# Stages of a tile two quads apart, three or four tiles to a group, and one-hots behind the steps of a slot, in a one-core graph, attention and slice-token kernel

## The reference, cut to what matters

```python
edge_index = jnp.stack([src, dst])                     # 100,000 edges, 6,250 nodes
xn = _layernorm(x, axis=-1)                            # x: 6250 x 256
x = x + gnn(xn, edge_index, ...) + mix(xn[None], ...)[0]
x = x + ffn(_layernorm(x, axis=-1)[None], ...)[0]

def _gnn_layer(x, row, col, W, b, g, beta):            # twice, W0 then W1
    neigh = x[col]
    agg = segment_sum(neigh, row, num_segments=n)      # sums of gathered rows
    h = (x + agg / deg) @ W.T + b
    hn = (h - mu) * rsqrt(var + EPS) * g + beta
    return silu(hn)
# ffn: logits -> softmax over 64 slices and 8 heads -> slice tokens -> attention -> back
slice_weights = softmax((x_mid @ W_slice + b_slice) / temp, axis=-1)
slice_token = einsum('bhnc,bhng->bhgc', fx_mid, slice_weights)
```

## Time and profile before

| | |
|---|---|
| time, median of 3 | 3014.8 us (3012.59 to 3029.4) |
| the profiled execution | 3023.39 us, span 3021.6 us |
| mean granted TensorE clock | 0.867 |
| busy share PE, PEld, DVE, ACT, POOL | 75%, 54%, 50%, 53%, 50% |
| gathers, all on POOL | 1568 |

### The profile page before, as it was taken

One profiled execution on the slowest core, in us unless ns is written; L12 is line 12 of the kernel. 1 busy time (PEld: TensorE's weight loads), 2 busy tenths in 40 slices (PEclk: granted clock), 3 DMA queues, 4 the chain that ended last, 5 costly groups with the idle time before them and its releaser, 6 DMA issues.

```text
span 3021.6 us, 35181 instructions
## 1 busy us (share of the span) xinstructions
PE 2264.3 (75%) x9037; PEld 1622.0 (54%) x9037; DVE 1504.1 (50%) x3513; ACT 1600.5 (53%) x3861; POOL 1522.8 (50%) x1591
## 2 busy tenths in 40 slices
PE   2376588778788788787669476768787877778699
PEld 1253366556565565565545354545454645555368
DVE  8899835555555555556127613343433334345511
ACT  5220276667667667666626465464554555565322
POOL 0000376566555656657740577576756676674000
PEclk9687699998999899999887787989887988889889
DMA  7110133233232333323361444243424343343322
GB/s 177 34 51 0 50 111 100 84 96 96 88 89 87 97 90 101 99 86 101 111 147 52 121 121 142 87 142 94 139 75 133 97 139 114 111 134 91 87 54 60
DMA packets 132041, 293.68 MB, mean 97 GB/s; under 512 B 31098, under 2 KB 76506, under 8 KB 128975
## 3 DMA queue, kind: packets, MB, share of 16 engines
q0 software_dynamic: 75584, 208.18, 23.6%
q1 hardware_dynamic: 17266, 44.84, 5.6%
q10 hardware_dynamic: 39000, 38.41, 4.2%
HBM read 259.31 MB, written 32.00 MB: 96 GB/s over the span
## 4 chain that ended last, share of the span: by engine, by line
PE 46%; DVE 25%; ACT 9%; POOL 8%; issue 7%; DMA 3%; ACTq 1%; DVEq 1%; SPq 0%; POOLq 0%
PE ps L1222 15%; POOL whole L671 8%; PE ps L1241 7%; DVE whole L1942 5%; PE ps L1376 4%; PE ps L1471 3%; DVE arena_a L1553 3%; ACT arena_b L782 3%; PE ps L1258 3%; DVE arena_a L1554 3%; PE ps L1381 2%; DMA arena_b<-mix_rows 2%; PE ps L1310 2%; PE ps L1239 1%; ACT whole L784 1%
## 5 line engine op out<-in xcount | busy, mean ns | idle before, releaser
L671 POOL DMA_INDIRECT whole<-table,arena_a x1568 | 1513.7, 965 | 1010.4 <-issue 457.1
L1222 PE MATMUL ps<-whole 128*125 x3968 | 1024.7, 412 | 210.3 <-issue 85.0
L1222 PEld LDWEIGHTS ps<-whole 128*125 128x125 f32 x3968 | 797.0, 205 | 394.2 <-issue 262.4
L1888 DVE TENSOR_TENSOR whole<-ps,whole 125x257 f32 (+1 forms) x496 | 210.4, 424 | 1091.7 <-PE ps L1222 1069.5
L782 ACT ACTIVATE arena_b<-iota_row,arena_a 128x125 f32<-128x125 f32 (+1 forms) x1984 | 600.4, 387 | 98.5 <-PE ps L1222 46.6
L784 ACT ACTIVATE whole<-arena_b,ones 128x1000 f32<-128x1000 f32 (+1 forms) x248 | 279.9, 1129 | 8.1
L1241 PE MATMUL ps<-arena_b,whole 128*125 128x384 f32 x400 | 225.9, 704 | 0.0
L1239 PE MATMUL ps<-arena_b,ones 3*125 3x384 bf16 x100 | 46.3, 463 | 164.8 <-ACTq L825 164.8
L1942 DVE RECIPROCAL whole<-whole 125x512 f32<-125x512 f32 x50 | 167.7, 3353 | 1.7
L812 ACT ACTIVATE whole<-whole 125x512 f32<-125x512 f32 x50 | 31.6, 631 | 251.4 <-DVE whole L1946 251.4
L1239 PEld LDWEIGHTS ps<-arena_b,ones 3*125 3x125 bf16 x100 | 15.3, 153 | 233.5 <-issue 233.5
(11 more groups left out here) (437 smaller groups left out, 3133.2 us busy)
## 6 DMA issues: line engine op xcount, KB each, us to landing
whole<-table,arena_a POOLq DMA_INDIRECT x1568, 2.8
table<-whole SPq DMA_DIRECT2D x9, 1120.0 KB
whole<-table ACTq DMA_DIRECT2D x50, 125.0 KB
mix_rows<-whole ACTq DMA_DIRECT2D x50, 125.0 KB
arena_a<-table ACTq DMA_DIRECT2D x50, 125.0 KB
arena_b<-in_x_dram ACTq DMA_DIRECT2D x50, 125.0 KB
arena_b<-mix_rows ACTq DMA_DIRECT2D x50, 125.0 KB
x_rows<-whole ACTq DMA_DIRECT2D x50, 125.0 KB
```

The costliest lines, as they stand in the source:

```text
L671: pool.indirect_dma_start(gat[:, GRP * slot + k, 0:D], None, table[l], bass.IndirectOffsetOnAxis(ap=s_dst[:, n:n + 1], axis=0)).then_inc(s ...
L1222: mm = pe.matmul(ps[0:PT, banks[at % len(banks)], 0:width], onehot[:, ROUND * (r % 2) + QS * k + n, :], gat[:, bass.ds(slots[QS * k + n], ...
L1888: dve.tensor_tensor(to, ps[0:PT, banks[at % len(banks)], 0:width].unsqueeze(1), to, ALU.add).then_inc(s("agg_added"), 1)
```

## The change

1. **The plan.** `GROUPS` goes from six tiles to four and, at the end, fewer: 16 groups in place of 12. A tick below 215 is "even": there a stage needs its predecessors two ticks back or more, not one, and a stage (other than S, R, V, Q) comes at most every fourth tick, not every tick. The costs are other numbers, the PE limit is 2.2 in place of 2.3, the DVE limit 2.4 while there are quads and 3.5 after, in place of 3.1.
2. **One-hots on ACT, layer two.** They stand behind the tick's steps and `move_rows`. The first four `Abs` of group tick/2 + 2 come in the even tick, the other four and the `Relu` in the odd one.
3. **`move_rows`** is called for the tick two before, not one.
4. **One-hots on ACT, layer one.** Two groups come ahead of slot 0, and group h + 2 comes behind slot h.

```diff
-GROUPS = [6, 6, 6, 6, 6, 6, 5, 4, 2, 1, 1, 1]
+GROUPS = [4] * 10 + [3, 2, 2, 1, 1, 1]
-PE_COST = {"W": 1.9, "L": 1.0, "D": 0.35, "H": 1.4, "T": 0.35}
-DVE_COST = {"N": 1.6, "M": 1.5, "X": 1.8, "Z": 1.1, "S": 1.5, "V": 1.5, "B": 0.45, "U": 0.6}
+PE_COST = {"W": 1.6, "L": 2.1, "D": 0.6, "H": 1.6, "T": 0.6}
+DVE_COST = {"N": 1.6, "M": 1.4, "X": 1.9, "Z": 1.0, "S": 1.3, "V": 1.3, "B": 0.45, "U": 0.5, "R": 0.2, "Q": 0.4}
+EVEN_UNTIL = 215
+EVEN_PACE = 4
+        even = tick < EVEN_UNTIL
+        dve_room = 2.4 if tick < NQ else 3.5
-                if any(at.get(one, tick) >= tick for one in need):
+                if any(at.get(one, tick) + (1 if even else 0) >= tick for one in need):
                     break
-                if items and (pe + PE_COST.get(st, 0) > 2.3 or dve + DVE_COST.get(st, 0) > 3.1):
+                if st not in "SRVQ" and k and tick - at[st, k - 1] < (EVEN_PACE if even else 1):
                     break
-                if any(s0 == st for s0, _ in items) and st not in "SRVQ":
+                if items and (pe + PE_COST.get(st, 0) > 2.2 or dve + DVE_COST.get(st, 0) > dve_room):
                     break
...
+                def first_half(grp):
+                    for k in range(GRP // 2):
+                        act.activation(away_b[:, k, :], iota_row[:, :], ACT.Abs, bias=s_row[:, grp * GRP + k:grp * GRP + k + 1])
+
-                    for k in range(GRP):
+                    for k in range(GRP // 2 if rest else 0, GRP):
...
-                    window(onehots_ahead, mix_slot)
+                    for grp in range(AHEAD):
+                        onehots(grp)
+                    for half in range(HALVES):
+                        if half < SLOTS:
+                            mix_slot(half)
+                        onehots_ahead(half)
...
-                        if tick % 2 == 0 and tick // 2 + AHEAD < NSG:
-                            onehots(tick // 2 + AHEAD)
                         set_up(tick)
                         for st, k in items:
                             second_step(st, k)
-                        for st, k in PLAN[tick - 1] if tick else []:
+                        for st, k in PLAN[tick - 2] if tick >= 2 else []:
                             move_rows(st, k)
+                        if tick // 2 + AHEAD < NSG:
+                            if tick % 2 == 0:
+                                first_half(tick // 2 + AHEAD)
+                            else:
+                                onehots(tick // 2 + AHEAD, rest=True)
```

More of the change, by code:

```diff
@@ L81 @@
 FED = {"tok": 1, "osT": 2, "attn": 3}
-GROUPS = [6, 6, 6, 6, 6, 6, 5, 4, 2, 1, 1, 1]
+GROUPS = [4] * 10 + [3, 2, 2, 1, 1, 1]
 assert sum(GROUPS) == NT
 STAGES = ("W", "N", "M", "L", "D", "C", "Q", "V", "X", "Z", "R", "S", "B", "H", "T", "U")
-PE_COST = {"W": 1.9, "L": 1.0, "D": 0.35, "H": 1.4, "T": 0.35}
-DVE_COST = {"N": 1.6, "M": 1.5, "X": 1.8, "Z": 1.1, "S": 1.5, "V": 1.5, "B": 0.45, "U": 0.6}
+AFTER = {"T": "U", "H": "T", "B": "H", "X": "Z", "D": "C", "L": "D", "M": "L", "N": "M", "W": "N", "R": "S", "Q": "V"}
+PE_COST = {"W": 1.6, "L": 2.1, "D": 0.6, "H": 1.6, "T": 0.6}
+DVE_COST = {"N": 1.6, "M": 1.4, "X": 1.9, "Z": 1.0, "S": 1.3, "V": 1.3, "B": 0.45, "U": 0.5, "R": 0.2, "Q": 0.4}
 X1_RING, BASE_RING, XL_RING = 3, 3, 3
+EVEN_UNTIL = 215
+EVEN_PACE = 4
 def second_layer_plan():
@@ L98, in second_layer_plan @@
     counts = {st: len(GROUPS) if st in "SRVQ" else NT for st in STAGES}
-    before = {"T": "U", "H": "T", "B": "H", "X": "Z", "D": "C", "L": "D", "M": "L", "N": "M", "W": "N", "R": "S", "Q": "V"}
     last_of = {"S": "B", "V": "X"}
     group_first = {"Z": "R", "C": "Q"}
-    room = {("U", 2): "T", ("Z", 2): "X", ("C", XL_RING): "W", ("T", 1): "H"}
+    room = {"U": (2, "T"), "Z": (2, "X"), "C": (XL_RING, "W"), "T": (1, "H")}
     tick = 0
     while nxt["W"] < NT:
+        even = tick < EVEN_UNTIL
+        dve_room = 2.4 if tick < NQ else 3.5
         pe, dve, items = 0.0, 0.0, []
@@ L109, in second_layer_plan @@
                 need = []
-                if st in before:
-                    need.append((before[st], k))
+                if st in AFTER:
+                    need.append((AFTER[st], k))
                 if st in last_of:
@@ L115, in second_layer_plan @@
                     need.append((group_first[st], group_of[k]))
-                for (other, n), done in room.items():
-                    if other == st and k >= n:
-                        need.append((done, k - n))
-                if any(at.get(one, tick) >= tick for one in need):
+                if st in room and k >= room[st][0]:
+                    need.append((room[st][1], k - room[st][0]))
+                if any(at.get(one, tick) + (1 if even else 0) >= tick for one in need):
                     break
@@ L774, in _, with onehots @@
             for l in range(2):
-                def onehots(grp, l=l):
+                def first_half(grp):
+                    for k in range(GRP // 2):
+                        act.activation(away_b[:, k, :], iota_row[:, :], ACT.Abs, bias=s_row[:, grp * GRP + k:grp * GRP + k + 1])
+                def onehots(grp, rest=False, l=l):
                     made = (grp - RG + 1) * (GRP // QS) + NQ * l
@@ L787, in onehots_ahead @@
                 def onehots_ahead(half):
-                    if half == 0:
-                        for grp in range(AHEAD):
-                            onehots(grp)
                     if half + AHEAD < NSG:
@@ L992, in _ @@
                             second_step(st, k)
-                        for st, k in PLAN[tick - 1] if tick else []:
+                        for st, k in PLAN[tick - 2] if tick >= 2 else []:
                             move_rows(st, k)
-                    assert all(st not in "UX" for st, k in PLAN[-1])
+                        if tick // 2 + AHEAD < NSG:
[3 more added lines that the diff above has]
+                                onehots(tick // 2 + AHEAD, rest=True)
+                    assert all(st not in "UX" for items in PLAN[-2:] for st, k in items)
             act.wait_ge(s("tail_made"), 1)
```

## The result

The changed kernel takes 2914.8 us (median of four runs, 2911.82 to 2919.37) against 3013.7 us for the kernel before on the same chip: a ratio of 0.9664 [0.9634, 0.9694], or 99 us less. The forecast was 2920, from a sum of 97 us less. The profiled execution took 2919.37 us with a span of 2917.3 and a mean granted clock of 0.879. In the changed file the gather is L674, SP's wait for used slots L617, the quads L1234, and the stages T, H, D, L and W on PE are L1368, L1372 and L1374, L1380, L1386 and L1388, and L1393. The columns of the first view are those of the earlier trace rows: the stretch of the quads, from there to the last W, and the end of the ffn.

The account below looks back on a forecast made before the run. POOL's gathers were taken as layer two's floor, 981 us, with only 105 us of stops to win. 105 us gained in the quads minus 8 us behind them made 97 us: 3014.8 - 97 = 2918, taken as 2920; low 2896, high 2980.

Parts of the forecast that it names:

- POOL's stops: Layer two's gathers: POOL's 104.6 us of waits on SP's free slots fall to 10 us, bounds 0 and 50.
- The last quads: End of layer two's quads: they end 14 us after POOL instead of 24, at 2692 us; bounds 10 and 24.
- After the quads: Stretch from the last quad to the last W: 8 us longer than its 75 us, bounds 0 and +25.
- Table loads: ACT in layer two: 54 loads instead of 40, 18 us more, hidden by ACT's slack.
- One-hots: ACT in layer two, one-hots placed behind the steps: 0 us, bounds -5 and +10.
- `move_rows`: ACT's queue issues, all one tick later: 0 us; next user at least ten ticks on in the even part.
- Layer one: ACT's one-hot order in layer one: 0 us in the stage's 1157 us, bounds -5 and +5.
- A: Layer two's quads: PE becomes the limit, 200 of its 260 us idle remain, 2963 us in all; chance 0.15.
- B: Layer two's quads: ACT's copies of T, H and D come late, 3053 us in all; chance 0.07.
- C: Layer two's gathers: a quarter slow down, costing 102 us, so no change at 3015 us; chance 0.06.
- the forecast's own range: Whole kernel: 2896 us (no stops, 10 us of last quads, no longer end) to 2950 us; forecast's chance 0.72.
- 153 us of waits in four kinds: PE in layer two's quads: waits of L on M, T on U and ACT's copies, 153 of 260 us idle, removed.

Follow-up runs that it names:

- ACT's part alone: Kernel before, old plan kept, with ACT's new one-hot order in both layers and move_rows two ticks back: 3067.37 us, ratio 1.0152.
- L and M apart: Kernel before, planner placing a tile's L only after the tick of the previous tile's M, D not ahead of that L: 2903.26 us, ratio 0.9621.
- plan-only kernel: Changed plan with ACT's order and move_rows of the kernel before: 2917.24 us, ratio 0.9658 to the kernel before.

## Why the prediction was right, point by point

**POOL's stops.** The main term, 104.6 us less 10, measured 104.6 less 0.6. POOL is done with its last gather at 2677.1 us (2676.2 + 0.95); forecast 2678. Yet I had left 10 us of stops, so 9 us are missing elsewhere. POOL's group in layer two, of the kernel before and of the changed one, shows where:

```profile
L671 POOL DMA_INDIRECT whole<-table,arena_a x784 | 749.1, 956 | 469.7 <-issue 232.5 <-DMA table<-whole 132.6 <-SPq L614 104.6
```

```profile
L674 POOL DMA_INDIRECT whole<-table,arena_a x784 | 750.7, 958 | 370.8 <-issue 237.9 <-DMA table<-whole 132.2 <-SPq L617 0.6
```

A stop in the list of waits is the whole gap between two gathers, its ordinary 0.30 us included. With the 21 stops went none of these gaps: issue rose from 232.5 to 237.9 us. That is 5.4 us that I took out with the stops and that stays, 1.6 us are in the gathers, and 1.2 us in the start of the stream (1687.9 against 1686.7). The two errors nearly cancel; that the end of POOL came out within 1 us is luck.

**The last quads.** 10.5 us behind POOL (2687.6 against 2677.1), at the good bound of 10 and not the 14 taken.

**After the quads.** +4.8 us, forecast +8, bounds 0 and +25. The one more W was right, but three more L and D are left, not two more L (40 and 28 records of L's 512 columns; 163 on PE in place of 135). PE's busy time still rose by only 4.8 us, since its records ran shorter, W's 414 ns in the mean in place of 495. With a spread from 61.1 us to 75.0 at almost the same count in other runs, that +8 came near is partly luck.

**Table loads.** 54 as counted, hidden as forecast; 32 loads take no less time. The Trainium skill (ScalarE: Activation LUTs, Table sets: the hidden batching unit) advises to batch by table set. Here that gained nothing (0.9668 with 32 loads, 0.9664 with 54); ACT is busy 604 of 984 us.

**One-hots.** 0 us forecast and 0 measured, alone on the old plan (0.9986, on the slower chip) and, together with `move_rows`, with the new one (0.9658 without, 0.9664 with). ACT's waits for the x2 store, which I said would go, are still 10.8 and 5.6 us; they cost nothing.

**`move_rows`.** 0 is right with the changed plan, and only there. The reason that I gave, that the next user is ten ticks on in the even part, fits both: it is eleven or more there, and three in 20 places of the old plan, where the same edit costs 1.8%. (The even part repeats itself every 40 ticks, eight tiles, and not every 20 and four as given ahead.)

**Layer one.** The records of layer one's quads start from 379.8 to 1563.9 us against 378.8 to 1562.2, 0.7 us longer; forecast 0. With ACT's part alone it is 380.4 to 1565.1.

**The rivals.** A, PE as the limit at 2963: PE's busy time went the other way, 834 to 778 us. I had taken it as fixed by the instructions. That is the one term wrong in kind: the granted clock rose from 0.86 to 0.89, and it did so as well in the kernel with L and M apart, whose stages still come in bursts. B, ACT's copies late: 27.7 us of such waits in all (17.0, 6.7, 2.8 and 1.2), against the 260 that it needs; of the 145 copies that I counted the changed plan has 137 in its quads. C, slow gathers: the median is 946 ns with DVE busy 402 of 984 us.

**The range.** I ended the forecast's own range at 2950, but its bounds add up to more: 3014.8 - 104.6 + 50 + 25 = 2985. The result lies inside both.

**What the prediction had too simple.** I put the kernel before within a tenth of POOL's floor and looked at POOL's 105 us as the thing to win. The number was right, but the bound was not POOL: an eighth fewer gathers gained only 17 us there. And I credited the gain to the whole of the plan, 153 us of waits in four kinds. The runs show that the rule against one kind, L with M in one tick, is enough, and that the second tick, the pace and the groups add nothing in the quads. That L and M apart is shown as enough does not show which share of it is the wait itself (83.3 us) and which the clock behind it (the 49 us between 834 and 785).

**The best version.** L and M apart on the kernel before: 2903.26 us, ratio 0.9621, with two more rules in the planner and the shortest stretch behind the quads of all. The changed kernel with stages one tick apart, 2909.44 us, is not told apart from it: their runs overlap.

## What to carry to other kernels

Where two engines walk one list in order, look for a pair of stages in one tick that hand over from the one to the other and back; a rule that parts that one pair may give all that a whole new schedule gives. To learn whether a producer is the bound, take an eighth of its work away: its busy share and its stops alone told here only how much room there was, and not what took it. A load moved one tick later cost nothing or 1.8% here, by the distance to its next user in the plan, so such an edit is priced with the plan that it goes with.

## What the hardware did that I had not expected

TensorE's busy time for nearly the same work in the same stretch was 834, 785, 778 and 752 us (before, L and M apart, changed, changed with fewer gathers), at a granted clock of 0.86, 0.89, 0.89 and 0.92. PE's idle time beside it was 260, 204, 206 and 132 us, but idle time alone does not give the clock: the plan-only kernel has 798 us of busy time at 0.87 with only 188 us idle, and ACT's part alone 826 us at 0.84 with 325. Four records of L took 3.10 us after a stop of 3.75 us, and 1.98 right behind two quads; the granted clock was 0.65 from 2184.1 to 2187.5 us in the first place and 1.00 in the second. So in tick 112 a wait on PE cost its own length and 1.1 us of the work behind it. What sets the clock of the whole stretch stays open.

The three chips do not agree: the kernel before has medians of 3019.51, 3017.2 and 3406.16 us on them.
